# Graph layers of a GNN + mixture-of-experts kernel: the tiles of nodes taken in eleven runs, heavy and light in turn, instead of in ascending order

## What is computed

```python
def _rgcn_conv(x, W, Wroot, b, src, dst, etype):      # 8 relations
    seg = dst * R + etype
    sums = segment_sum(x[src], seg, N * R)
    cnt = segment_sum(ones, seg, N * R)
    mean = (sums / maximum(cnt, 1)).reshape(N, R, -1)
    return x @ Wroot + b + einsum('nrd,rde->ne', mean, W)

h = relu(_rgcn_conv(layernorm(x), ..., W1))
x = x + _rgcn_conv(h, ..., W2)
z = layernorm(x)                                       # then, for the two best experts of a row:
x = x + sum_e weight_e * (gelu(z @ W1[e] + b1[e]) @ W2[e] + b2[e])
```

## Time and profile before

| | us |
|---|---|
| median of 3 runs | 3500.47 (3499.16 to 3519.07) |
| span of the profiled execution | 3064.4 |
| median less that span | 436.1 |
| TensorE busy in the span | 2352.2 |
| GpSimd busy in the span | 1836.5 |
| mean granted TensorE clock | 0.879 |

### The profile page before, as it was taken

One profiled execution on the slowest core, in us unless ns is written; L12 is line 12 of the kernel. 1 busy time (PEld: TensorE's weight loads), 2 busy tenths in 40 slices (PEclk: granted clock), 3 DMA queues, 4 the chain that ended last, 5 costly groups with the idle time before them and its releaser, 6 DMA issues.

```text
span 3064.4 us, 82720 instructions
## 1 busy us (share of the span) xinstructions
PE 2352.2 (77%) x19212; PEld 1776.0 (58%) x19213; DVE 1782.2 (58%) x4944; ACT 1167.6 (38%) x2306; POOL 1836.5 (60%) x1908
## 2 busy tenths in 40 slices
PE   1456777778888887456777888888987189999999
PEld 0123444555666775123445556667776178888888
DVE  7434445555566664333445555656666278877777
ACT  5001223334445553011223344455542165655554
POOL 1777777766666553777777777666536623333333
PEclk9556789999999998557899999999995599999999
DMA  7343333333333321333343444333335432322222
GB/s 244 100 130 105 108 108 108 109 101 99 97 94 93 90 88 58 106 99 115 115 119 118 123 122 125 112 113 111 106 110 192 146 123 86 100 72 72 72 72 61
DMA packets 164416, 331.14 MB, mean 108 GB/s; under 512 B 35518, under 2 KB 101786, under 8 KB 164216
## 3 DMA queue, kind: packets, MB, share of 16 engines
q0 software_dynamic: 90864, 245.38, 26.9%
q1 hardware_dynamic: 39608, 41.02, 4.5%
q10 hardware_dynamic: 33872, 43.92, 4.5%
HBM read 283.29 MB, written 49.07 MB: 108 GB/s over the span
## 4 chain that ended last, share of the span: by engine, by line
PE 48%; POOL 24%; issue 15%; DVE 7%; DMA 3%; DVEq 2%; ACT 1%; POOLq 0%; SPq 0%; ACTq 0%
POOL ring L450 20%; PE more_banks L1254 15%; PE sum_banks L1392 8%; PE sum_banks L1234 7%; PE sum_banks L1235 5%; PE sum_banks L1382 4%; PE more_banks L1382 4%; POOL lot_in L470 3%; PE more_banks L1246 3%; DMA ring<-table,row_tab 2%; DVE sel L890 1%; DMA out<-edge_work,lot_ids 1%; PE more_banks L1366 1%; DVEq L881 1%; DVE weights L1072 0%
## 5 line engine op out<-in xcount | busy, mean ns | idle before, releaser
L450 POOL DMA_INDIRECT ring<-table,row_tab x1568 | 1509.2, 963 | 703.8 <-issue 339.0
L1254 PE MATMUL more_banks<-weights,stage 128*128 128x256 f16 x5292 | 846.9, 283 | 7.8 <-ACT stage L561 4.5
L589 ACT ACTIVATE stage<-sum_banks,inv 128x256 f16<-128x256 f32 x784 | 327.4, 471 | 815.5 <-DVE inv L923 398.7
L1254 PEld LDWEIGHTS more_banks<-weights,stage 128*128 128x128 f16 x5292 | 502.4, 101 | 144.9 <-issue 71.6
L1234 PE MATMUL sum_banks<-ring,sel 128*128 x1568 | 449.3, 287 | 161.1 <-DVE sel L890 84.2
L898 DVE TENSOR_SCALAR sel_more<-lane,win_off,key_tab 128x128 f16 x780 | 268.8, 345 | 443.4 <-SPq L355 371.2
L1234 PE MATMUL sum_banks<-ring,sel_more 128*128 x780 | 244.3, 314 | 350.0 <-DVE sel_more L898 193.8
L890 DVE SCALAR_TENSOR_TENSOR sel<-lane,win_off,key_tab 128x256 f16<-128x256 f16 x792 | 349.4, 482 | 240.4 <-PE more_banks L1254 235.8
L1235 PE MATMUL sum_banks<-ring,sel 128*128 x1568 | 448.7, 287 | 0.0
L561 ACT ACTIVATE stage<-more_banks 128x1024 f16<-128x1024 f16 x392 | 402.7, 1027 | 15.1 <-PE more_banks L1246 14.9
L1234 PEld LDWEIGHTS sum_banks<-ring,sel_more 128*128 x780 | 78.4, 100 | 529.7 <-issue 524.9
(11 more groups left out here) (287 smaller groups left out, 2763.0 us busy)
## 6 DMA issues: line engine op xcount, KB each, us to landing
ring<-table,row_tab POOLq DMA_INDIRECT x1568
weights<-L_ffn_W ACTq DMA_DIRECT2D x96, 178.5 KB
stage<-L_ffn_W ACTq DMA_DIRECT2D x16, 1024.0 KB, 5.5
edge_work<-lot_in SPq DMA_DIRECT2D x54, 260.0 KB, 2.7
table<-edge_work SPq DMA_DIRECT2D x7, 896.0 KB, 4.4
table<-edge_work ACTq DMA_DIRECT2D x49, 128.0 KB
out<-acc SPq DMA_DIRECT2D x6, 1024.0 KB
acc<-x SPq DMA_DIRECT2D x6, 896.0 KB, 11.0
```

The source lines that it names most:

```text
L450: pool.indirect_dma_start(ring_rows[:, b % RING, 0:2 * D], None, tables[layer], bass.IndirectOffsetOnAxis(row_tab[:, b:b + 1], 0)).then_in ...
L589: act.activation(mean16[:, slot, h, 0:D], ps_sum[slot][h][:, 0:D], ACT.Copy, scale=inv[:, ds(c * 2 + h, 1)]).then_inc(mean_high[layer], 1)
L1254: return [pe.matmul(ps_out[par], rows[:, xp * KD + k, :], w16[:, wp, k, r * D:(r + 1) * D], start=part == 0 and n == 0, stop=part == PARTS ...
```

## The change

The tiles are renumbered: position p in the work is node tile `ORDER[p]`. Eleven runs, six with many edges (0; 1; 2, 3; 4 to 6; 7 to 9; 10 to 12) and five with few (13 to 24; 25 to 31; 32 to 37; 38 to 42; 43 to 48) alternate. A block that two runs share is gathered for both, so a layer has `GATHERS` = 794 gathers and not 784. Everything on chip that is indexed by tile is in the new order: x, the layer norm's rows, `win_off`, `meta`, `row_tab`, `key_tab`, `free_meta`. Loads and stores of x, of the first table and of the result are cut at the seams of the runs. The second layer's table is written at `tile_at[t]`, which ScalarE loads into a register for each tile. Matmuls per tile and the loops' structure are unchanged.

```diff
+    RUNS = ((0, 1), (13, 25), (1, 2), (25, 32), (2, 4), (32, 38), (4, 7), (38, 43), (7, 10), (43, 49), (10, 13))
+    COUNT = len(RUNS)
+    ORDER = [t for a, b in RUNS for t in range(a, b)]
+    TAIL = ORDER.index(TILES - 1)
+    GATHERS = BLOCKS + COUNT - 1
+    MASK = (1 << (GATHERS + 3 * WINDOWS).bit_length()) - 1
...
@@ SyncE: loads and stores cut at seams; the ring
-                sp.dma_start(acc[:, at:at + tiles, :], x[...]).then_inc(x_in[c], 16)
+                for a, b, t in whole(c * CHUNK, (c + 1) * CHUNK):
+                    sp.dma_start(acc[:, a:b, :], x[...]).then_inc(x_in[c], 16)
...
+                for a, b, t in pieces(c * CHUNK, (c + 1) * CHUNK):
+                    sp.dma_start(tables[0][...], rows16[:, a:b, :]).then_inc(table1_out, 16)
...
+                def freed(s):
+                    sp.wait_ge(steps_done[layer], sp.snap(regs[s], donate=True) & MASK)
+                    sp.sem_inc(slots_free[layer], 1)
...
@@ GpSimd: constants run by run; gathers
+            for r, (a, b) in enumerate(RUNS):
+                pool.iota(id_all[...]); pool.iota(look_no[...]); pool.memset(...); pool.memset(...)
+                pool.iota(win_off[...])
...
-            pool.wait_ge(rows_tab, 1)
+            pool.memset(row_src[:, BLOCKS:], 0.0).then_inc(order_set, 1)
+            pool.wait_ge(tabs_set, COUNT + 1)
...
-                for b in range(BLOCKS):
+                for b in range(GATHERS):
...
-                    pool.indirect_dma_start(ring_rows[:, b % RING, 0:2 * D], None, tables[layer],
+                    pool.indirect_dma_start(ring_rows[:, (b + 2) % RING, 0:2 * D], None, tables[layer],
...
@@ ScalarE: row and key tables put in the order of the runs, one copy of 784 columns per run and table
+            act.wait_ge(runs_ready, 1)
+            act.load(run_regs, run_tab[0:1, :])
+            for r in range(COUNT):
+                act.activation(row_tab[:, ds(run_to[r], BLOCKS)], row_src[:, ds(run_from[r], BLOCKS)], ACT.Copy).then_inc(tabs_set, 1)
+                act.wait_ge(tabs_set, r + 2)
             (the four copies of last_row and first_row, as before)
+            for r in range(COUNT):
+                act.activation(key_tab[:, ds(run_to[r], BLOCKS)], key_src[:, ds(run_from[r], BLOCKS)], ACT.Copy).then_inc(tabs_set, 1)
+                act.wait_ge(tabs_set, COUNT + r + 2)
...
+                    act.load([tile_reg], tile_at[0:1, ds(t, 1)])
                     act.wait_ge(row_low, t + 1)
...
@@ VectorE: last windows first, then the runs, then the rest
             chunk_low(CHUNKS - 2)
+            for q in range(Q):
+                ins = v.tensor_scalar(ends_later[:, q, :], look_no[0:NAT, :], last_win[0:NAT, q:q + 1], None, ALU.is_gt)
+            ins.then_inc(later_ready, 1)
...
+            v.wait_ge(spans_ps, 1)
+            (six short operations: start, length and place of each run, to run_tab)
+            v.sem_inc(runs_ready, 1)
+            chunk_low(CHUNKS - 1)
+            for q in range(Q):
+                ins = v.tensor_scalar(starts_later[:, q, :], look_no[0:NAT, 0:WINDOWS], first_win[0:NAT, q:q + 1], None, ALU.is_ge)
...
-            v.tensor_copy(meta[0:1, 0:WINDOWS, 0], lo)
+            for r in range(COUNT):
+                v.tensor_scalar(meta[0:1, wins, 0], lo[:, wins], run_shift[:, r:r + 1], 2.0, ALU.add, ALU.add)
+                v.tensor_scalar(run_end[:, r + 1:r + 2], upto[:, last - 1:last], 2.0 * last, None, ALU.add)
...
-            link(v.tensor_tensor_scan(free_meta[0:1, :], one_row, turn_row, 0.0, ALU.add, ALU.add))
+            link(v.tensor_tensor_scan(free_src[:, 0:BLOCKS], one_row, turn_row, 0.0, ALU.add, ALU.add))
+            (six linked operations on rows of the eleven runs)
+            v.load(run_regs, run_tab[0:1, :])
+            v.wait_ge(tabs_set, COUNT + 1)
+            for r in range(COUNT):
+                link(v.tensor_scalar(free_row[:, ds(to[r], BLOCKS)], free_src[:, ds(of[r], BLOCKS)], run_steps[:, r:r + 1], run_end[:, r + 1:r + 2], ALU.add, ALU.min))
+            link(v.tensor_copy(free_meta[0:1, :], free_row[:, 0:GATHERS]))
+            v.wait_ge(tabs_set, 2 * COUNT + 1)
+            for r in range(1, COUNT):
+                ins = v.tensor_scalar(first, first, ..., ..., ALU.max, ALU.min)       # one column of key_tab
             v.sem_inc(setup_done, 1)
...
@@ VectorE's loop of extra blocks
-                        v.wait_ge(rows_ready[layer], block + 1)
+                        v.wait_ge(rows_ready[layer], (lo & MASK) + i + 3)
...
@@ TensorE's loop of extra blocks; need is lo + 2
-                            pe.wait_ge(more_ready[layer], since + i + 1)
-                            block = (lo + i + 2).with_bounds(min_val=0, max_val=BLOCKS - 1)
-                            add_block(to, flat(sel_more[:, ds(block & (RING - 1), 1), :]), block, False, True).then_inc(steps_done[layer], 1)
+                            pe.wait_ge(more_ready[layer], (since & MASK) + i + 1)
+                            add_block(to, flat(sel_more[:, ds((need + i) & (RING - 1), 1), :]), need + i + 2, False, True).then_inc(steps_done[layer], 1)
...
-                        pe.wait_ge(rows_ready[layer], lo[j] + 2)
+                        pe.wait_ge(rows_ready[layer], need[j] & MASK)
```

More of the change, by code:

```diff
@@ L37, in build_program @@
     AHEAD = RING // 2
-    TURNS = BLOCKS // RING
+    RUNS = ((0, 1), (13, 25), (1, 2), (25, 32), (2, 4), (32, 38), (4, 7), (38, 43), (7, 10), (43, 49), (10, 13))
+    COUNT = len(RUNS)
+    ORDER = [t for a, b in RUNS for t in range(a, b)]
+    TAIL = ORDER.index(TILES - 1)
+    assert sorted(ORDER) == list(range(TILES))
+    assert [r for r in sorted(RUNS)] == list(RUNS[0::2] + RUNS[1::2])
+    AT = [sum(b - a for a, b in RUNS[:r]) for r in range(COUNT + 1)]
+    GATHERS = BLOCKS + COUNT - 1
+    TURNS = (GATHERS - RING) // RING
+    OVER = GATHERS - RING - TURNS * RING
+    USES = [len(range(s, GATHERS, RING)) for s in range(RING)]
+    LOOKS = WINDOWS + 2 * COUNT
     PITCH = 2 * D + 4
+    MASK = (1 << (GATHERS + 3 * WINDOWS).bit_length()) - 1
     WSH, KSH = WIN.bit_length() - 1, P.bit_length() - 1
@@ L67, in build_program, with pieces, whole @@
     WAYS = CHUNK + 1
-    STORES = (TILES - 1) // 8 + 1
-    assert (TILES - 1) % 8 == 0
+    def pieces(first, last):
+        cuts = [(max(AT[r], first), min(AT[r + 1], last)) for r in range(COUNT)]
+        return [(a, b, ORDER[a]) for a, b in cuts if a < b]
+    def whole(first, last):
+        return [p for p in pieces(first, min(TAIL, last)) + pieces(max(TAIL + 1, first), last)]
+    STORES = len(whole(0, TILES)) + 1
     tables = [nc.dram_tensor(f"table{l}", [NP, 2 * D], f16, kind="Internal").ap() for l in range(2)]
@@ L265, in build_program @@
         routed, zs_ready = sem("routed"), sem("zs_ready")
[L266 removed]
+        assert len(set(USES[0:GROUPS])) == 1
+        spots_after = 16 * USES[0] * 2
         scattered = gathered[0:GROUPS]
@@ L439, in _ @@
                 pool.sem_inc(place_free, 1)
-            pool.wait_ge(rows_tab, 1)
+            pool.wait_ge(tabs_ps, 1)
+            pool.wait_ge(wins_ready, 1)
+            pool.memset(row_src[:, BLOCKS:], 0.0).then_inc(order_set, 1)
+            pool.wait_ge(tabs_set, COUNT + 1)
             pool.wait_ge(ring_ones, 1)
-            pool.wait_ge(table1_out, 16 * CHUNKS)
+            pool.wait_ge(table1_out, 16 * sum(len(pieces(c * CHUNK, (c + 1) * CHUNK)) for c in range(CHUNKS)))
             for layer in range(2):
@@ L1013, in _ @@
                 v.memset(cells[:, 0:5, :], 0.0)
-            for i in range(CHUNK):
-                v.tensor_scalar(ids7[:, i:i + 1], part_no[:], float(i * P), None, ALU.add)
             v.tensor_scalar(valid, part_no[:], float(LAST), None, ALU.is_lt)
@@ L1199, in _ @@
             pe.wait_ge(later_ready, 1)
-            for a in range(2):
-                for q in range(Q):
-                    ins = pe.matmul(bank[4 + a][:, 0:WINDOWS], ones16[0:NAT, :], later[:, a, q, :], start=q == 0, stop=q == Q - 1)
+            for q in range(Q):
+                ins = pe.matmul(bank[4][:, 0:LOOKS], ones16[0:NAT, :], ends_later[:, q, :], start=q == 0, stop=q == Q - 1)
+            ins.then_inc(spans_ps, 1)
+            pe.wait_ge(later_ready, 2)
+            for q in range(Q):
+                ins = pe.matmul(bank[5][:, 0:WINDOWS], ones16[0:NAT, :], starts_later[:, q, :], start=q == 0, stop=q == Q - 1)
             ins.then_inc(spans_ps, 1)
```

185 lines of the change are left out of this document (122 added, 63 removed).

## The result

| | before | after |
|---|---|---|
| median of 4 runs each | 3508.09 (3499.16 to 3519.07) | 3678.67 (3676.93 to 3680.73) |
| span of the profiled execution | 3064.4 | 3675.0 |
| mean granted TensorE clock | 0.879 | 0.824 |

The changed kernel takes 1.0487 times as long, interval 1.0460 to 1.0513: 170 us slower. The forecast was 3512 us, in a range up to 3570.

The account below looks back on a forecast made before the run. Gathers and TensorE's extra steps were both taken as near their limit in heavy tiles. Stock -20, loops +12, set-up +18 and the rest +2 us gave a 3076.4 us span, plus 436 us 3512, range 3460 to 3570.

Parts of the forecast that it names:

- What bounds the kernel: Heavy tiles: gathers every 1.25 us and TensorE's extra steps every 1.11 us are both near their limit.
- Cover: in tile 0 of layer 1 the gathers hide it: Tile 0 of layer 1: the gathers hide the register operations added to the loops of extra blocks.
- Register work in the loops: Extra-block loops of TensorE and VectorE: 0.015 us a step, +12 us, between -5 and +78.
- Set-up: VectorE's chain before the first selection matmul grows by 18 us, from 13 to 28; TensorE starts at 115.
- Stock in front of heavy runs: Rows gathered ahead in light runs shorten the heavy runs that follow: -20 us, between -6 and -45.
- Ten more gathers: One more gather at each seam, 12.5 us of GpSimd a layer beside full rings: 0, at most +10 us.
- The sum: Span of the profiled execution: 3064.4 - 20 + 12 + 18 + 2 = 3076.4 us.
- I keep that: The runs' median lies 436 us above the profiled span; added to the forecast span it gives 3512 us.
- B, slower by the loop: Rival: added register operations lift the extra step from 1.11 to 1.21 us or more; 3565 us, chance 0.16.
- C, slower by the clock: Rival: TensorE's clock makes the changed kernel slower, priced at 32 us; chance 0.10.
- A, clearly faster: Rival: the 0.5 us between steps is partly waiting for VectorE's lists; 3394 us, half the gain 3435; chance 0.14.

Follow-up runs that it names:

- 16-bit kernel before: The kernel before with its three tables of register values stored as 16-bit instead of 32-bit numbers, nothing else: 3867.7 us, 1.1030 of before.
- the run with four more: The changed kernel with four more register operations in each extra step of TensorE, the value unchanged: 3846.7 us, 1.0930 of before.
- The three pairs on one chip: Eleven runs against natural order: changed kernel 3689.3 and 3704.0 us, with named masks 3633.3 and 3618.3, with 16-bit tables and no masks 3911.5 and 3898.7.

## Why the prediction was wrong

*What bounds the kernel.* "Both resources are near their limit" held for the execution that was traced. Ordinary executions seem to lie elsewhere: in the 16-bit kernel before, with the pitch still at 1.11 us, tiles 1 to 5 of layer 1 take 269 us for 162 gathers of 1.25 us, 203 in all, and GpSimd waits 87 us of it for slots. TensorE's slower register loads are 17 us of the 269. So the gathers are not the bound there, and an addition to the extra steps arrives in full (34 us for 121 steps). That the kernel before with its 32-bit tables behaves so too is argued and not shown. "Cover: in tile 0 of layer 1 the gathers hide it" was right in its effect: the masks cost 5 us of a possible 29 there. What covers them wasn't followed up; GpSimd had waits for slots there too.

*Register work in the loops: this is the step that failed.* The prediction took 0.015 us a step, 12 us, with 0.1 us a step as its upper end, "since the operations replace others nearly one for one". The runs show 0.29 us a step on TensorE (1.11 to 1.40) and 0.26 on VectorE (0.74 to 1.00), and 167 us for the kernel before with such edits alone. Two things were wrong. The operations don't replace others: the traces have ten register instructions and a branch in TensorE's turn, where the kernel before has seven and a branch (one move, one ALU instruction and one fused register instruction more), and eight in VectorE's, where it was five. And bounds were at hand: a turn before had seven register instructions and a branch in a pitch of 1.11 us, 0.5 of it idle. That is 0.06 us for each of the eight if only the idle time is theirs, 0.14 if the whole pitch is; the run with four more showed 0.088. Three more would have been 0.19 to 0.42 us a step, 146 to 325 us in all, where the text had -5 to +78.

*Set-up.* +18 us forecast, with the first matmul at 115; it came at 119.5, 22 us later than the earlier trace rows. Right within its range; ScalarE's copies of 784 columns left every 1.0 us, as worked out. The 0.2 us of a short linked operation has its measure in the trace of before, 0.19 (VectorE's starts at 85.04, 85.23 and 85.42), and the load of 22 registers, counted as 1.4, took 1.83. Where the 4 us above the count lie wasn't followed up.

*Stock in front of heavy runs.* -20 us forecast. The three pairs on one chip give -28, +1 and -1 once the longer set-up is taken off, so whether the term was right is open; it is not what failed. *Ten more gathers:* nothing was forecast, and no run has them apart; GpSimd has 874 us of waits for slots to put them in. That these waits would stay near 269 was wrong with the loop term, and before's 294 may not be typical either: its 16-bit form, without masks, has 1062 us.

*The sum.* On one chip the kernel before with the register arithmetic alone takes 3677.3 us and the changed kernel 3680.4. So the loops' 167 us are nearly all of the loss, and set-up, order and gathers together add 3 us, although the first matmul comes 21 us later. What gives the difference back isn't known, and with 16-bit tables the same parts cost 43.8 us. No version tried is faster than the kernel before.

*"I keep that"*: the 436 us between span and median were carried over as a constant, and the span forecast at 3076. The span came at 3675, 2 us below its run. The 436 us were not something outside the span, but time inside it that the one traced execution didn't have. As a constant in the sum it did little harm; but it was the sign that the trace isn't one of a typical execution, and that rows near a limit may stand on its other side.

*Rivals.* B, slower by the loop, was the right mechanism, with its condition ("from about 0.05 us a step") exceeded sixfold. It had a chance of 0.16, and its times of up to 3588 rested on the same 0.1 us a step; the 3565 that it was given lies between that and half the price. C, slower by the clock: the clock does swing with the runs, but its mean is 0.817 in the changed kernel and 0.825 in the kernel before with the change's loops beside it, and their times are the same. It had a chance of 0.10 and was priced at 32 us, which no run shows as a term: the trace has a swing from 0.65 in a heavy run to 1.00 in a light one, and no pair that differs in the order alone has the eleven runs slower by more than their set-up and a microsecond or two. A, clearly faster, needed sequencer gaps that were waits for lists; they were register work, since TensorE's pitch stays at 1.40 when VectorE's step goes from 1.00 to 1.27. Its time for half the gain, 3435, doesn't come out of its own terms: 3500 less 69 plus 32 is 3463.

## What to carry to other kernels

Count the register instructions of a loop's turn before and after an edit, and price each new one between the idle time and the whole pitch divided by their number: here 0.09 us each in 780 turns, where three of them cost more than the reordering for which they were added was forecast to win. Compare a profiled span with the timed runs first. Where it is far below them, no argument should rest on two rates that lie within that gap of each other, as 1.11 and 1.25 did here.

## What the runs showed of the hardware

- One more register instruction in the loop of extra blocks costs 0.088 us of pitch on TensorE (1.40 to 1.75 for four) and 0.068 on VectorE (1.00 to 1.27 for four), while the trace gives TensorE's instruction a duration of 0.032 us.
- A register load of one tile's numbers takes 1.36 us on TensorE from a 32-bit table and 4.73 us from a 16-bit table; in the 98 loads from the 16-bit table (3.48 to 4.97 us each) matmuls start only in the first 1.84 us, and the next one 0.46 us after a load's end at the earliest. A load of four registers takes 0.33 and 0.99 us.
- Register instructions stall for about 0.7 us, 247 to 328 times on TensorE in fourteen executions of versions of this kernel, some of them on two engines at once; the one execution without such stalls was 12% shorter than the timed runs of its kernel, which is more than the stalls of any trace add up to.
